# Two score phases per batch in place of four, with scores and transposes of the probabilities in the same four PSUM banks

## The chip, the core and the metric

The kernel runs on one NeuronCore of one Trainium2 chip. Its engines work from instruction streams of their own and meet at semaphores: TensorE (PE in the profile; its weight loads stand as PEld), VectorE (DVE), ScalarE (ACT), GpSimd (POOL) and SyncE (SP), which here only issues DMAs. The metric is the device time of one execution in microseconds, the median over several runs; lower is better.

## What is computed

64 graphs ("batches") of 256 nodes with 512 features, one 0/1 adjacency matrix for all. Two layers, each a residual with a layer norm behind it: a graph convolution, then masked attention with 8 heads of 64.

```python
def reference(x, adj, ...):
    # layer 0
    mi, mj = x @ Wi.T, x @ Wj.T
    a = adj.astype(x.dtype); deg = a.sum(axis=1)
    h = layernorm(x + deg[None, :, None] * (mi + b) + einsum('ij,bjo->bio', a, mj))
    # layer 1
    q, k, v = (split_heads(h @ W.T + bias) for W, bias in ((Wq, bq), (Wk, bk), (Wv, bv)))
    scores = where(adj == 0, -inf, einsum('bhqd,bhkd->bhqk', q, k) / 8)
    out = einsum('bhqk,bhkd->bhqd', softmax(scores), v)       # heads joined again
    return layernorm(h + out @ Wo.T + bo)
```

## The kernel before, in words

**Precision.** Every operand of a matmul is kept as two rounded halves, `_hi` and `_lo`; a product is three matmuls (hi·hi, lo·hi, hi·lo). ACT copies a PSUM result into the `_hi` half, DVE subtracts that from PSUM into the `_lo` half. `P` is 128, `R` = 2 row tiles of 128 nodes, `C` = 4 feature chunks, `G` = 4 pairs of heads; `g` counts the pairs.

**The step.** `steps` (L166) runs `step(b)` for b = 0 to 62, a loop of two steps a turn for most of them, and then `last_step(63)`. One step overlaps three batches: the attention of batch b, layer 0 and the projections q, k, v of batch n = b + 1, and the output projection y of batch b - 1. Every engine has its own list of calls for the step, written out by hand (PE L494, ACT L646, DVE L848, POOL L302). These lists and the semaphores set the order of everything; nothing schedules.

**PE.** `mj`, `mi` (L352, L363) multiply xT with two weights; `aggregate` (L370) applies the adjacency matrix; `transpose_h` (L404) turns the normalised h; `q`, `k`, `v`, `y` are projections of 12 matmuls of 512 columns (24 of 256 for a half of q or k). All of these write the three banks `proj`. `scores(b, g)` (L452) is 12 matmuls with 64 rows each, in six pairs that run side by side in the upper and the lower half of the array, one head in each; they fill the two banks `score`. `transpose_p(b, g, i)` (L469) turns the normalised probabilities of one head into bank `pt[i]`. `attend(b, g)` (L480) multiplies them with `v_both` into the bank `av`; it waits until `pt_low` (DVE, L791) has made both `pT_lo` of pair g, and until `o_sum` (L796) has read `av` of the pair before.

**The softmax of a pair.** `maxima` (DVE, L769: mask, row maxima, then `exp_bias`, a tensor_scalar), `exponentials` (ACT, L608), `inverse_sums` (DVE, L787), `normalise_even` (ACT, L618) and `normalise_odd` (POOL, L244), `transpose_p`, `pt_high` (ACT, L626), `pt_low`, `attend`, `o_low_part` (ACT, L633), `o_sum`, `o_high` (ACT, L640), `split_o` (POOL, L278).

**The norm of h.** `mi_sum`, `agg_sum` (DVE, L808, L817) add up h, `norm_stats` and `norm_mean` (L832, L836) take mean and variance, `root("h", n)` (POOL, L269) makes `rstd_h` with two small operations, and `norm_apply` (DVE, L842) scales the two row tiles of h with a tensor_scalar each (L845), from SBUF to SBUF. `transpose_h` waits for both.

**The next x.** `xT_high` and `split_xT` (POOL, L235, L251) make the two halves of xT for batch b + 2, one operation over 128x1024 elements each; their data is in SBUF a step early (`load_xT`, L183).

The calls between which the work around the change lies, on POOL and on DVE:

```python
305                normalise_odd(b, 0)
306                root("h", n)
307                normalise_odd(b, 1)
308                normalise_odd(b, 2)
309                if ahead: xT_high(b + 2)
310                if ahead: split_xT(b + 2)
...
862                norm_mean("h", n)
863                maxima(b, 2)
864                norm_apply("h", n, h_row)
```

## Time and profile before

| | |
|---|---|
| Median of 3 runs | 3143.62 us (3142.37 to 3143.76) |
| The profiled execution | 3145.57 us, its span 3143.7 us |
| PE busy | 3096.7 us, 99% of the span |
| DVE / ACT / POOL busy | 2298.9 / 1691.2 / 1148.2 us (73 / 54 / 37%) |
| Chain that ended last | PE 98%, DVE 1% |
| Granted TensorE clock, mean | 0.993 |

The profile is of one execution, from the first instruction to the last. A matmul's end in it is modelled: successive matmuls overlap, so the distance from start to start says how fast PE goes, not the duration of one. "Idle before <-releaser" is how long the engine stood before an instruction and what let it go on. A row with x2 merges two like instructions, its duration reaching from the start of the first to the end of the last.

### The profile page before, as it was taken

How to read it: one execution, taken by the hardware profiler on the slowest of the kernel's cores; microseconds unless marked ns; L12 is line 12 of the kernel's file. 1: busy time of each engine (PE TensorE's matmuls, PEld its weight loads, DVE VectorE, ACT ScalarE, POOL GpSimd, SP SyncE). 2: the span in 40 equal slices, each digit the busy share in tenths (PEclk: the TensorE clock that was granted, in tenths of full speed). 3: DMA queues.
4: the chain of work that ended last, by engine and by line, in shares of the span. 5: the costliest groups of instructions: out<-in, count | busy, mean ns of one | idle time of the engine just before them, and what ended most of it. 6: DMA issues, size and time to landing. Idle time of an engine off the chain costs nothing.

```text
span 3143.7 us, 60262 instructions
## 1 busy us (share of the span) xinstructions
PE 3096.7 (99%) x20480; PEld 2694.0 (86%) x20480; DVE 2298.9 (73%) x5644; ACT 1691.2 (54%) x4487; POOL 1148.2 (37%) x1097
## 2 busy tenths in 40 slices
PE   6999999999999999999999999999999999999997
PEld 5888888888888888888888888888888888888886
DVE  5677777777777777777777777777777777777776
ACT  3555555555555555555555555555555555555554
POOL 2343333333433333333334333333343333333332
PEclk8999999999999999999999999999999999999998
DMA  3011011010010110110101101101001011011010
GB/s 127 15 41 40 20 40 40 20 40 27 33 40 20 40 40 20 40 40 21 40 20 40 40 20 40 40 20 40 30 30 40 20 40 40 20 40 40 20 34 21
DMA packets 73002, 108.36 MB, mean 34 GB/s; under 512 B 3600, under 2 KB 36880, under 8 KB 72976
## 3 DMA queue, kind: packets, MB, share of 16 engines
q1 hardware_dynamic: 72976, 108.02, 10.4%
q8 instruction: 15, 0.25, 0.0%
q14 instruction: 11, 0.09, 0.0%
HBM read 74.46 MB, written 33.55 MB: 34 GB/s over the span
## 4 chain that ended last, share of the span: by engine, by line
PE 98%; DVE 1%; issue 0%; ACT 0%; DMA 0%; POOL 0%; POOLq 0%; DVEq 0%; SPq 0%; ACTq 0%
PE proj L337 73%; PE av L337 8%; PE pt L476 7%; PE score L463 7%; PE proj L414 2%; DMA probs<-in_w0T 0%; DVE h L845 0%; DVE probs L778 0%; DVE pT_lo L793 0%; DVE oT L802 0%; DVE wj_lo L897 0%; DVE wq_lo L897 0%; POOL var_eps_h L272 0%; DVE stats_out L834 0%; ACT probs L614 0%
## 5 line engine op out<-in xcount | busy, mean ns | idle before, releaser
L614 ACT ACTIVATE probs<-probs,exp_bias 128x256 f32<-128x256 f32 x1024 | 508.6, 498 | 374.5 <-DVE exp_bias L784 374.5
L280 POOL TENSOR_TENSOR oT_lo<-oT,oT_hi 128x256 fp32r<-128x256 f32 x256 | 189.2, 739 | 977.1 <-ACT oT_hi L644 977.1
L247 POOL TENSOR_TENSOR probs<-probs,row_inv 128x512 f32<-128x512 f32 x256 | 266.8, 1042 | 494.6 <-DVE row_inv L789 494.6
L778 DVE CUSTOM_DVE_ANT_0 probs<-score,mask_add 128x256 f32<-128x256 f32 x1024 | 371.4, 420 | 92.2 <-PE score L463 42.5
L630 ACT CAST pT_hi<-pt 128x512 fp32r<-128x512 f32 x512 | 280.1, 587 | 169.8 <-PE av L337 112.8
L793 DVE TENSOR_TENSOR pT_lo<-pt,pT_hi 128x512 fp32r<-128x512 f32 x512 | 333.5, 681 | 20.2 <-ACT pT_hi L630 16.2
L802 DVE SCALAR_TENSOR_TENSOR oT<-av,bv_cols,o_part 64x256 f32<-64x256 f32 x512 | 243.3, 475 | 97.2 <-ACT o_part L637 69.0
L784 DVE TENSOR_SCALAR exp_bias<-row_max 128x4 f32<-128x4 f32 x256 | 297.5, 1162 | 8.9
L623 ACT ACTIVATE probs<-probs,row_inv 128x256 f32<-128x256 f32 x512 | 234.2, 509 | 117.2 <-DVE row_inv L789 117.2
L337 PE MATMUL proj<-hT_hi,wq_hi 128*128 128x256 f32 x1024 | 289.2, 282 | 1.5 <-DVE hT_lo L739 1.5
L337 PE MATMUL proj<-hT_hi,wq_lo 128*128 128x256 f32 x1024 | 288.9, 282 | 0.0
L337 PE MATMUL proj<-hT_lo,wq_hi 128*128 128x256 f32 x1024 | 288.8, 282 | 0.0
L337 PE MATMUL proj<-hT_hi,wk_lo 128*128 128x256 f32 x1024 | 287.9, 281 | 0.0
L337 PE MATMUL proj<-hT_hi,wk_hi 128*128 128x256 f32 x1024 | 287.5, 281 | 0.0
L337 PE MATMUL proj<-hT_lo,wk_hi 128*128 128x256 f32 x1024 | 287.5, 281 | 0.0
L476 PE MATMUL pt<-ident,probs 128*128 128x128 f32 x2048 | 281.8, 276 | 2.1 <-ACT probs L623 2.1
L337 PE MATMUL av<-pT_hi,v_both 128*128 128x256 f32 x1024 | 272.0, 298 | 4.2 <-DVE pT_lo L793 4.2
L337 PE MATMUL av<-pT_lo,v_both 128*128 128x256 f32 x1024 | 256.0, 283 | 0.0
L476 PEld LDWEIGHTS pt<-ident,probs 128*128 128x128 f32 x2048 | 233.3, 141 | 20.1 <-ACT probs L623 2.6
L573 ACT CAST v_both<-proj 128x512 fp32r<-128x512 f32 x128 | 68.9, 590 | 334.6 <-PE av L337 330.5
L758 DVE SCALAR_TENSOR_TENSOR k_lo<-proj,bk_cols,k_hi 128x256 fp32r<-128x256 f32 x256 | 112.1, 479 | 169.4 <-ACT k_hi L598 169.4
L739 DVE TENSOR_TENSOR v_both<-proj,v_both 128x512 fp32r<-128x512 f32 x128 | 82.6, 686 | 208.0 <-ACT v_both L573 208.0
(100 smaller groups left out, 8897.3 us busy)
## 6 DMA issues: line engine op xcount, KB each, us to landing
xT_raw<-in_xT SPq DMA_DIRECT2D x64, 512.0 KB, 4.5
xb<-in_x SPq DMA_DIRECT2D x64, 512.0 KB, 5.3
out<-hb SPq DMA_DIRECT2D x64, 512.0 KB, 3.3
probs<-in_w0T SPq DMA_DIRECT2D x1, 1024.0 KB, 6.8
hb<-in_w0T SPq DMA_DIRECT2D x1, 1024.0 KB, 9.0
probs<-in_wqT SPq DMA_DIRECT2D x1, 1024.0 KB, 5.5
hb<-in_wkT SPq DMA_DIRECT2D x1, 1024.0 KB, 6.3
probs<-in_wvT SPq DMA_DIRECT2D x1, 1024.0 KB, 5.3
```

Source lines behind the costliest of these rows:

```text
L247: pool.tensor_tensor(probs[:, g % 2, 1, :, :], probs[:, g % 2, 1, :, :], row_inv[:, g % 2, R:2 * R].unsqueeze(2).to_broadcast([P, R, N]), ...
L280: pool.tensor_tensor(oT_lo[:, g, :], oT[:, :], oT_hi[:, g, :].bitcast(F32), ALU.subtract).then_inc(o_split, 1)
L337: return pe.matmul(dst, lhsT, rhs, start=start, stop=stop)
L463: last = pe.matmul(score[i][:, r * N:(r + 1) * N], q_[home, g, r * P:(r + 1) * P], k_[home, g, :], start=(r == 0 and j == 0), stop=(j == l ...
L476: last = pe.transpose(dst[:, kt, r * P:(r + 1) * P], probs[:, g % 2, i, r, kt * P:(kt + 1) * P], ident[:, :])
L614: last = nc.scalar.activation(e, e, ACT.Exp, bias=exp_bias[:, g % 2, s:s + 1], scale=SCALE, accum_out=row_sum[:, g % 2, s:s + 1])
L623: last = nc.scalar.activation(e, e, ACT.Copy, scale=row_inv[:, g % 2, r:r + 1])
L630: nc.scalar.copy(pT_hi[:, i, :, :], pt[i][:, :].rearrange("p (k q) -> p k q", k=R)).then_inc(pt_hi_done, 1)
L778: last = V.tensor_tensor_reduce(out=probs[:, g % 2, i, r, :], in0=score[i][:, r * N:(r + 1) * N], in1=mask_add[:, r, :], scale=1.0, scalar ...
L784: V.tensor_scalar(exp_bias[:, g % 2, :], row_max[:, g % 2, :], MAX_FLOOR, -SCALE, ALU.max, ALU.mult).then_inc(bias_done, 1)
L793: V.tensor_tensor(pT_lo[:, i, :, :], pt[i][:, :].rearrange("p (k q) -> p k q", k=R), pT_hi[:, i, :, :].bitcast(F32), ALU.subtract).then_in ...
L802: last = V.scalar_tensor_tensor(out=oT[i * HALF:(i + 1) * HALF, :], in0=av[0:HALF, i * N:(i + 1) * N], scalar=bv_cols[:, 2 * g + i:2 * g + ...
```

## The change

- The banks `score[0..1]` and `pt[0..1]` become four banks `attn[0..3]`. Pair g has the two banks `attn[2 * (g % 2) + i]`: first for its scores, then, once the probabilities have been read out, for its transposes. `pT_hi` and `pT_lo` get a second buffer for odd g. To make room, `hT_hi` and `hT_lo` take the place of `mj_hi` and `mj_lo`, which are dead when they are written.
- `scores(b, pair)` makes the scores of two pairs of heads, 24 matmuls in a row, so that a step has two score phases and not four: one in the place of the old first one, the other behind `attend(b, 1)`. It waits for `pt_low` of the pairs that had the banks before.
- On PE `y(b - 1, 0)` stands between the transposes of pairs 0 and 1, `y(b - 1, 1)` and `transpose_h` between `attend(b, 0)` and `attend(b, 1)`. q and k follow in a row behind the second score phase.
- ACT, DVE and POOL call the same functions in a new order. `last_step` is reordered in the same manner on all four engines (`scores(b, 0)`, y, pairs 0 and 1, y, `scores(b, 1)`, pairs 2 and 3).

No instruction that computes is added or taken away.

```diff
@@ -89,8 +89,9 @@
         mj_lo = sb("mj_lo", [P, R, D], F32R)
         h = sb("h", [P, R, D])
         hb = sb("hb", [P, 2, R, D])
-        hT_hi = sb("hT_hi", [P, C, N], F32R)
-        hT_lo = sb("hT_lo", [P, C, N], F32R)
+        hT_hi = mj_hi[:, :, :].rearrange("p r (a n) -> p (r a) n", a=2)
+        hT_lo = mj_lo[:, :, :].rearrange("p r (a n) -> p (r a) n", a=2)
@@ -100,8 +101,8 @@
         k_lo = sb("k_lo", [P, C, N], F32R)
         v_both = sb("v_both", [P, R, HEADS, 2 * DH], F32R)
         probs = sb("probs", [P, 2, 2, R, N])
-        pT_hi = sb("pT_hi", [P, 2, R, N], F32R)
-        pT_lo = sb("pT_lo", [P, 2, R, N], F32R)
+        pT_hi = sb("pT_hi", [P, 2, 2, R, N], F32R)
+        pT_lo = sb("pT_lo", [P, 2, 2, R, N], F32R)
         o_part = sb("o_part", [HALF, 2, N])
         oT = sb("oT", [P, N])
         oT_hi = sb("oT_hi", [P, G, N], F32R)
@@ -127,8 +128,8 @@
         proj = [bank(f"proj{i}") for i in range(3)]
-        score = [bank(f"score{i}") for i in range(2)]
-        pt = [bank(f"pt{i}") for i in range(2)]
+        attn = [bank(f"attn{i}") for i in range(4)]
         av = bank("av")
@@ -303,15 +304,15 @@
                 n = b + 1
                 add_bias(n)
                 normalise_odd(b, 0)
+                normalise_odd(b, 1)
                 root("h", n)
-                normalise_odd(b, 1)
-                normalise_odd(b, 2)
                 if ahead: xT_high(b + 2)
                 if ahead: split_xT(b + 2)
                 split_o(b, 0)
+                split_o(b, 1)
+                normalise_odd(b, 2)
                 normalise_odd(b, 3)
                 if y_: root("out", b - 1)
-                split_o(b, 1)
                 split_o(b, 2)
                 residual(n, 1 - parity, stored=y_)
                 split_o(b, 3)
...
@@ -449,28 +450,28 @@
                     pe.wait_ge(read["k"], 2 * n + 2)
                 rows_times_w("v", r, hT_hi, hT_lo, "wv")
-            def scores(b, g, first=False):
-                pe.wait_ge(read["q"], 2 * b + g // 2 + 1)
-                pe.wait_ge(read["k"], 2 * b + g // 2 + 1)
-                if not (first and g == 0):
-                    pe.wait_ge(max_done, 2 * (G * b + g))
-                terms = [(q_hi, k_hi), (q_lo, k_hi), (q_hi, k_lo)]
-                for r in range(R):
-                    for j, (q_, k_) in enumerate(terms):
-                        for i in range(2):
-                            home = slice(i * HALF, (i + 1) * HALF)
-                            last = pe.matmul(score[i][:, r * N:(r + 1) * N], q_[home, g, r * P:(r + 1) * P],
-                                             k_[home, g, :], start=(r == 0 and j == 0),
-                                             stop=(j == len(terms) - 1), skip_group_check=True)
-                            if r == R - 1 and j == len(terms) - 1:
-                                last.then_inc(score_done, 1)
-            def transpose_p(b, g, i, first=False):
+            def scores(b, pair, first=False):
+                pe.wait_ge(read["q"], 2 * b + pair + 1)
+                pe.wait_ge(read["k"], 2 * b + pair + 1)
+                if not (first and pair == 0):
+                    pe.wait_ge(pt_read, 2 * (G * b + 2 * pair))
+                for g in (2 * pair, 2 * pair + 1):
+                    terms = [(q_hi, k_hi), (q_lo, k_hi), (q_hi, k_lo)]
+                    for r in range(R):
+                        for j, (q_, k_) in enumerate(terms):
+                            for i in range(2):
+                                home = slice(i * HALF, (i + 1) * HALF)
+                                last = pe.matmul(attn[2 * (g % 2) + i][:, r * N:(r + 1) * N],
+                                                 q_[home, g, r * P:(r + 1) * P], k_[home, g, :],
+                                                 start=(r == 0 and j == 0), stop=(j == len(terms) - 1),
+                                                 skip_group_check=True)
+                                if r == R - 1 and j == len(terms) - 1:
+                                    last.then_inc(score_done, 1)
+            def transpose_p(b, g, i):
                 pe.wait_ge((norm_even_done, norm_odd_done)[i], G * b + g + 1)
-                if not (first and g == 0):
-                    pe.wait_ge(pt_read, 2 * (G * b + g) + i - 1)
-                dst = pt[i][:, :].rearrange("p (k q) -> p k q", k=R)
+                dst = attn[2 * (g % 2) + i][:, :].rearrange("p (k q) -> p k q", k=R)
                 for kt in range(R):
                     for r in range(R):
                         last = pe.transpose(dst[:, kt, r * P:(r + 1) * P],
...
@@ -497,32 +498,30 @@
                 scores(b, 0, not y_)
                 mj(n, 1)
                 mi(n, 0)
-                scores(b, 1)
                 mi(n, 1)
                 aggregate(n, 0)
                 aggregate(n, 1)
-                transpose_p(b, 0, 0, not y_)
-                transpose_p(b, 0, 1, not y_)
-                scores(b, 2)
+                transpose_p(b, 0, 0)
+                transpose_p(b, 0, 1)
                 if y_: y(b - 1, 0)
+                transpose_p(b, 1, 0)
+                transpose_p(b, 1, 1)
+                attend(b, 0, not y_)
                 if y_: y(b - 1, 1)
                 transpose_h(n, 0)
                 transpose_h(n, 1)
-                scores(b, 3)
-                transpose_p(b, 1, 0)
-                transpose_p(b, 1, 1)
-                attend(b, 0, not y_)
+                attend(b, 1)
+                scores(b, 1)
                 q(n, 0)
                 q(n, 1)
+                k(n, 0)
+                k(n, 1)
                 transpose_p(b, 2, 0)
                 transpose_p(b, 2, 1)
-                attend(b, 1)
-                k(n, 0)
-                k(n, 1)
+                v(n, 0)
                 transpose_p(b, 3, 0)
+                transpose_p(b, 3, 1)
                 attend(b, 2)
-                transpose_p(b, 3, 1)
-                v(n, 0)
                 v(n, 1)
                 attend(b, 3)
...
@@ -625,10 +622,11 @@
             def pt_high(b, g, i, first=False):
                 act.wait_ge(pt_done, 2 * (G * b + g) + i + 1)
-                if i == 0 and not (first and g == 0):
-                    act.wait_ge(av_done, G * b + g)
-                nc.scalar.copy(pT_hi[:, i, :, :],
-                               pt[i][:, :].rearrange("p (k q) -> p k q", k=R)).then_inc(pt_hi_done, 1)
+                if i == 0 and not (first and g < 2):
+                    act.wait_ge(av_done, G * b + g - 1)
+                nc.scalar.copy(pT_hi[:, g % 2, i, :, :],
+                               attn[2 * (g % 2) + i][:, :].rearrange("p (k q) -> p k q",
+                                                                     k=R)).then_inc(pt_hi_done, 1)
             def o_low_part(b, g, first=False):
                 act.wait_ge(av_done, G * b + g + 1)
@@ -648,36 +646,36 @@
                 mj_high(n, 0)
                 exponentials(b, 0)
                 mj_high(n, 1)
+                exponentials(b, 1)
                 normalise_even(b, 0)
-                exponentials(b, 1)
+                normalise_even(b, 1)
                 pt_high(b, 0, 0, not y_)
-                normalise_even(b, 1)
                 pt_high(b, 0, 1, not y_)
-                exponentials(b, 2)
+                o_low_part(b, 0, not y_)
+                pt_high(b, 1, 0, not y_)
+                pt_high(b, 1, 1, not y_)
                 hT_high(n, 0)
                 hT_high(n, 1)
+                o_low_part(b, 1)
+                o_high(b, 0, not y_)
+                exponentials(b, 2)
+                o_high(b, 1)
+                q_high(n, 0)
+                exponentials(b, 3)
                 normalise_even(b, 2)
-                pt_high(b, 1, 0)
-                pt_high(b, 1, 1)
-                o_low_part(b, 0, not y_)
-                exponentials(b, 3)
-                q_high(n, 0)
                 q_high(n, 1)
-                o_high(b, 0, not y_)
-                o_low_part(b, 1)
+                k_high(n, 0)
+                normalise_even(b, 3)
                 pt_high(b, 2, 0)
                 pt_high(b, 2, 1)
-                normalise_even(b, 3)
-                k_high(n, 0)
                 k_high(n, 1)
-                o_high(b, 1)
                 pt_high(b, 3, 0)
                 pt_high(b, 3, 1)
                 o_low_part(b, 2)
+                o_high(b, 2)
+                o_low_part(b, 3)
                 v_high(n, 0)
                 v_high(n, 1)
-                o_high(b, 2)
-                o_low_part(b, 3)
                 o_high(b, 3)
             def split_weight(i):
...
@@ -790,8 +789,9 @@
             def pt_low(b, g, i):
                 dve.wait_ge(pt_hi_done, 2 * (G * b + g) + i + 1)
-                V.tensor_tensor(pT_lo[:, i, :, :], pt[i][:, :].rearrange("p (k q) -> p k q", k=R),
-                                pT_hi[:, i, :, :].bitcast(F32), ALU.subtract).then_inc(pt_read, 1)
+                V.tensor_tensor(pT_lo[:, g % 2, i, :, :],
+                                attn[2 * (g % 2) + i][:, :].rearrange("p (k q) -> p k q", k=R),
+                                pT_hi[:, g % 2, i, :, :].bitcast(F32), ALU.subtract).then_inc(pt_read, 1)
             def o_sum(b, g, first=False):
@@ -847,50 +847,50 @@
             def step(b, parity, y_=True, ahead=True):
                 n, other = b + 1, 1 - parity
+                mj_low(n, 0)
                 maxima(b, 0, not y_)
-                mj_low(n, 0)
-                mi_sum(n, 0)
+                maxima(b, 1, not y_)
                 mj_low(n, 1)
                 inverse_sums(b, 0)
-                maxima(b, 1, not y_)
+                mi_sum(n, 0)
+                inverse_sums(b, 1)
                 mi_sum(n, 1)
                 agg_sum(n, 0)
                 agg_sum(n, 1)
                 norm_stats("h", n, 0, read["agg"], h_row)
                 norm_stats("h", n, 1, read["agg"], h_row)
-                inverse_sums(b, 1)
                 norm_mean("h", n)
-                maxima(b, 2)
+                pt_low(b, 0, 0)
+                pt_low(b, 0, 1)
                 norm_apply("h", n, h_row)
                 if y_: y_sum(b - 1, 0, other)
-                pt_low(b, 0, 0)
-                pt_low(b, 0, 1)
+                o_sum(b, 0, not y_)
+                pt_low(b, 1, 0)
+                pt_low(b, 1, 1)
                 if y_: y_sum(b - 1, 1, other)
-                inverse_sums(b, 2)
                 hT_low(n, 0)
                 hT_low(n, 1)
+                maxima(b, 2)
+                o_sum(b, 1)
                 maxima(b, 3)
+                q_low(n, 0)
                 if y_: norm_stats("out", b - 1, 0, read["y"], hb_row[other])
-                pt_low(b, 1, 0)
-                pt_low(b, 1, 1)
-                o_sum(b, 0, not y_)
+                inverse_sums(b, 2)
+                if y_: norm_stats("out", b - 1, 1, read["y"], hb_row[other])
+                if y_: norm_mean("out", b - 1)
                 inverse_sums(b, 3)
-                if y_: norm_stats("out", b - 1, 1, read["y"], hb_row[other])
-                q_low(n, 0)
                 q_low(n, 1)
-                o_sum(b, 1)
+                if y_: norm_apply("out", b - 1, hb_row[other])
+                k_low_half(n, 0)
                 pt_low(b, 2, 0)
                 pt_low(b, 2, 1)
-                if y_: norm_mean("out", b - 1)
-                k_low_half(n, 0)
                 k_low_half(n, 1)
                 pt_low(b, 3, 0)
+                pt_low(b, 3, 1)
                 o_sum(b, 2)
-                pt_low(b, 3, 1)
-                if y_: norm_apply("out", b - 1, hb_row[other])
+                o_sum(b, 3)
                 v_low(n, 0)
                 v_low(n, 1)
-                o_sum(b, 3)
             def split_weight(i):
                 dve.wait_ge(w_hi_done, i + 1)
...
```

What now stands in a row, at two places. **POOL, from `normalise_odd(b, 0)` (probs) through `root("h", n)` (var_eps_h, rstd_h) to the split of the next x (xT_hi, xT_lo).** Before:

```order
L247 TENSOR_TENSOR probs<-probs,row_inv 128x512
L271 ISA
L272 TENSOR_TENSOR var_eps_h<-mean_var_h,eps_cols 128x2
L275 TENSOR_TENSOR rstd_h<-var_eps_h,power_cols 128x2
L246 REGISTER_ALU
L247 TENSOR_TENSOR probs<-probs,row_inv 128x512
L246 REGISTER_ALU
L247 TENSOR_TENSOR probs<-probs,row_inv 128x512
L237 ISA
L239 REGISTER_ALU
L240 TENSOR_TENSOR xT_hi<-xT_raw,zero 128x1024
L253 TENSOR_TENSOR xT_lo<-xT_raw,xT_hi 128x1024
```

And after:

```order
L248 TENSOR_TENSOR probs<-probs,row_inv 128x512
L247 REGISTER_ALU
L248 TENSOR_TENSOR probs<-probs,row_inv 128x512
L272 ISA
L273 TENSOR_TENSOR var_eps_h<-mean_var_h,eps_cols 128x2
L276 TENSOR_TENSOR rstd_h<-var_eps_h,power_cols 128x2
L238 ISA
L240 REGISTER_ALU
L241 TENSOR_TENSOR xT_hi<-xT_raw,zero 128x1024
L254 TENSOR_TENSOR xT_lo<-xT_raw,xT_hi 128x1024
```

The two operations on xT stood behind two normalisations that had to wait for their pairs; now they stand right behind `rstd_h`.

**DVE, from the end of `maxima(b, 2)` (exp_bias) through `norm_apply` (h) to `hT_low`.** Before:

```order
L784 TENSOR_SCALAR exp_bias<-row_max 128x4
L845 TENSOR_SCALAR h<-h,mean_var_h,rstd_h 128x512 x2
L824 ISA
L826 TENSOR_TENSOR hb<-proj,hb 128x512
L793 TENSOR_TENSOR pT_lo<-pt,pT_hi 128x512 x2
L824 REGISTER_ALU
L826 TENSOR_TENSOR hb<-proj,hb 128x512
L788 REGISTER_ALU
L789 RECIPROCAL row_inv<-row_sum 128x4
L739 TENSOR_TENSOR hT_lo<-proj,hT_hi 128x512 x2
```

And after (`hT_lo` bears the name `mj_lo`, whose place it has taken):

```order
L840 BN_AGGR mean_var_h<-stats_h 128x2 x2
L792 TENSOR_TENSOR pT_lo<-attn,pT_hi 128x512 x2
L845 TENSOR_SCALAR h<-h,mean_var_h,rstd_h 128x512 x2
L824 ISA
L826 TENSOR_TENSOR hb<-proj,hb 128x512
L802 SCALAR_TENSOR_TENSOR oT<-av,bv_cols,o_part 64x256 x2
L792 TENSOR_TENSOR pT_lo<-attn,pT_hi 128x512 x2
L824 REGISTER_ALU
L826 TENSOR_TENSOR hb<-proj,hb 128x512
L737 TENSOR_TENSOR mj_lo<-proj,mj_hi 128x512 x2
```

`maxima(b, 2)` is gone from between `norm_mean` and `norm_apply`, and behind `norm_apply` now stand `o_sum(b, 0)` and the two `pt_low` of pair 1.

## Rows read from the trace of the kernel before

**Rows 1.** The page: busy time by engine, granted clock in 40 slices, the chain.
```profile
PE 3096.7 (99%) x20480; PEld 2694.0 (86%) x20480; DVE 2298.9 (73%) x5644; ACT 1691.2 (54%) x4487; POOL 1148.2 (37%) x1097
PEclk8999999999999999999999999999999999999998
PE 98%; DVE 1%; issue 0%; ACT 0%; DMA 0%; POOL 0%; POOLq 0%; DVEq 0%; SPq 0%; ACTq 0%
```

**Rows 2.** The chain in order of time: start us, us, what; two starts of `mj(n, 0)`.
```profile
1507.80 2.80 PE proj L337 x12
1510.60 0.91 PE score L463 x12
...
1523.06 0.87 PE pt L476 x8
...
1541.90 5.68 PE proj L337 x48
...
1555.95 2.80 PE proj L337 x12
```

**Rows 3.** Timeline of PE around `scores(b, 0)`: start us, us, engine, line, what.
```profile
1509.97 0.40 PE L337 MATMUL proj<-wj_hi,xT_lo 128*128 128x512 f32 x1
1510.20 0.39 PE L337 MATMUL proj<-wj_lo,xT_hi 128*128 128x512 f32 x1
1510.53 0.38 PE L463 MATMUL score<-k_hi,q_hi 64*128 64x256 f32 x2
1510.75 0.28 PE L463 MATMUL score<-k_hi,q_lo 64*128 64x256 f32 x2
...
1511.22 0.28 PE L463 MATMUL score<-k_lo,q_hi 64*128 64x256 f32 x2
1511.43 0.50 PE L337 MATMUL proj<-wj_hi,xT_hi 128*128 128x512 f32 x1
1511.77 0.39 PE L337 MATMUL proj<-wj_hi,xT_lo 128*128 128x512 f32 x1
```

**Rows 4.** Timeline of DVE and POOL in the same step, the norm of h.
```profile
1523.10 0.69 DVE L820 TENSOR_TENSOR h<-proj,h 128x512 f32<-128x512 f32 x1 [0.24 <-PE proj L337]
1525.09 0.31 DVE L840 BATCH_NORM_AGGREGATE mean_var_h<-stats_h 128x2 f32<-128x6 f32 x2
1525.76 0.70 POOL L275 TENSOR_TENSOR rstd_h<-var_eps_h,power_cols 128x2 f32<-128x2 f32 x1
1526.42 1.04 POOL L247 TENSOR_TENSOR probs<-probs,row_inv 128x512 f32<-128x512 f32 x1
1527.40 1.00 DVE L845 TENSOR_SCALAR h<-h,mean_var_h,rstd_h 128x512 f32<-128x512 f32 x2
1528.32 0.68 DVE L826 TENSOR_TENSOR hb<-proj,hb 128x512 f32<-128x512 f32 x1
1528.92 1.27 DVE L793 TENSOR_TENSOR pT_lo<-pt,pT_hi 128x512 fp32r<-128x512 f32 x2
1532.53 1.89 POOL L240 TENSOR_TENSOR xT_hi<-xT_raw,zero 128x1024 fp32r<-128x1024 f32 x1
1534.50 2.39 POOL L253 TENSOR_TENSOR xT_lo<-xT_raw,xT_hi 128x1024 fp32r<-128x1024 f32 x1
```

**Rows 5.** The same timeline later: `exp_bias` beside `xT_lo`, then `o_sum(b, 1)` and `pt_low`.
```profile
1535.09 1.83 DVE L784 TENSOR_SCALAR exp_bias<-row_max 128x4 f32<-128x4 f32 x1
1542.56 0.97 DVE L802 SCALAR_TENSOR_TENSOR oT<-av,bv_cols,o_part 64x256 f32<-64x256 f32 x2 [0.62 <-ACT o_part L637]
1543.56 1.29 DVE L793 TENSOR_TENSOR pT_lo<-pt,pT_hi 128x512 fp32r<-128x512 f32 x2
```

**Rows 6.** Timeline ahead of step 0: `root`, `norm_apply`, `xT_high(1)`, `split_xT(1)`.
```profile
33.99 0.70 POOL L275 TENSOR_TENSOR rstd_h<-var_eps_h,power_cols 128x2 f32<-128x2 f32 x1
34.66 1.89 POOL L240 TENSOR_TENSOR xT_hi<-xT_raw,zero 128x1024 fp32r<-128x1024 f32 x1
34.73 4.58 DVE L845 TENSOR_SCALAR h<-h,mean_var_h,rstd_h 128x512 f32<-128x512 f32 x2 [0.87 <-POOL rstd_h L275]
36.64 2.40 POOL L253 TENSOR_TENSOR xT_lo<-xT_raw,xT_hi 128x1024 fp32r<-128x1024 f32 x1
```

**Rows 7.** Stretches, us: PE, PEld, DVE, ACT, POOL busy, granted clock, DMA share, GB/s.
```profile
79.50:82.30 2.80, 0.00 (x0) 0.00 (x0) 2.74 (x14) 1.56 (x4) 1.91 (x3) 1.00 0.00 0
82.40:89.10 6.70, 6.06 (x32) 5.51 (x33) 3.82 (x10) 3.77 (x12) 4.54 (x3) 0.50 0.00 0
3097.80:3099.70 1.90, 0.00 (x0) 0.00 (x0) 1.51 (x4) 1.05 (x3) 1.36 (x2) 1.00 0.00 0
3099.80:3109.90 10.10, 6.01 (x34) 5.10 (x35) 4.96 (x24) 7.04 (x23) 4.48 (x5) 0.50 0.00 0
```

54 lines of the change are left out of this document (26 added, 28 removed).

## The prediction

> **What bounds the kernel now.** First the page: PE is busy 99% of the span, and the chain that ended last is 98% PE [rows 1]. In the chain in order of time a step runs from one `mj(n, 0)` to the next, 1507.80 to 1555.95: 48.15 us, every piece of it PE and none of it a wait [rows 2]. So a shorter step means either fewer microseconds of PE work, or nothing; and any wait that the new order puts in front of PE is paid in full. The granted clock is full in all slices but the first and the last [rows 1].
>
> **What the change takes away.** The timeline around `scores(b, 0)` shows what a score phase costs. Two 512-column matmuls start 0.23 us apart, the pairs of score matmuls 0.118 (1510.75 to 1511.22 over four). From the last `mj` matmul before the phase (1510.20) to the second one behind it (1511.77) are 1.57 us; without the phase it would be 2 x 0.233 = 0.47. The phase costs 1.10, its six pairs 6 x 0.118 = 0.71, and the rest, 0.39, is four gaps of about 0.1 where PE goes over from 128-row to 64-row matmuls and back (1510.20 to 1510.53, 1510.53 to 1510.75, 1511.22 to 1511.43, 1511.43 to 1511.77) [rows 3]. Four phases become two, and the 12 matmuls of the second pair then follow at 0.118 a pair: 2 x 0.39 = 0.78 us a step. The other matmuls and transposes are the same in number and kind, so PE's own work is 48.15 - 0.78 = 47.37 us a step. Over 63 steps that would be 49 us.
>
> **What it puts in.** I lay out the new step from the start of `mj(n, 0)` = 0, with the pieces of rows 2 and the distances of rows 3. PE: `mj(n, 0)` to 2.8, the score phase to 4.5, `mj(n, 1)`, `mi`, `aggregate` to 14.88, transposes of pair 0 to 15.75, `y(b-1, 0)` to 18.55, transposes of pair 1 to 19.42, `attend(b, 0)` to 20.37, `y(b-1, 1)` to 23.17, `transpose_h` to 24.04, and then `attend(b, 1)`, which needs the two `pt_low` of pair 1.
>
> DVE: `agg_sum(n, 1)` starts 0.20 behind the end of `aggregate` (before: 1523.10 against transposes from 1522.90 on), so at 15.08; from there to the end of `norm_mean` are 2.30 us [rows 4], 2.25 without the reciprocal that has moved away: 17.33. Then the two `pt_low` of pair 0, 1.27, whose data ACT has ready (transposes done at 15.9, two copies of 0.5): to 18.6.
>
> POOL: `rstd_h` ends 1.06 behind `norm_mean` (1525.40 to 1526.46) and POOL's next operation has started 0.04 before that [rows 4]. That next one is now `xT_high`. Nothing holds it: x lies ready since the step before, `mi` has ended at 13.2. So `xT_high` runs from 18.35 and `split_xT`, 1.97 behind it, from 20.32 to 22.71 [rows 4].
>
> `norm_apply` waits for `rstd_h`, so on DVE it can't start before 18.39, and meets `xT_high` in flight. What then happens stands in the prologue, where POOL and DVE have the same three calls in the same order: `xT_hi` starts 34.66, `norm_apply` 34.73, and its two instructions take 4.58 us and end at 39.31, 0.27 behind the end of `xT_lo` at 39.04 [rows 6]; undisturbed they take 1.00 [rows 4]. The tensor_scalar stands still while a POOL operation runs, and the second instruction comes behind the second operation. The loop has it too: `exp_bias`, four elements wide, takes 1.83 us and ends with `xT_lo` (1536.89) [rows 4, 5]. In the step of before `norm_apply` came between two POOL operations and nobody waited. By rows 6 the new one ends at 22.71 + 0.27 = 22.98.
>
> The Trainium skill has this as a rule (SBUF — State Buffer, section "Who interferes with whom"): VectorE in a two-port mode, which tensor_scalar can enter, and GpSimd take one pair of SBUF ports in turn, and the one that starts second blocks for the whole instruction. By that rule the 4.58 us of the prologue are no accident of the prologue; the trace agrees.
>
> Behind it on DVE are queued, at the spacings of rows 4 and 5: `y_sum` (starts 22.90, 0.60), `o_sum(b, 0)` (23.50, 1.00), two `pt_low` of pair 1 (24.50, 1.29), which end at 25.8. PE wants `attend(b, 1)` at 24.04 and starts it at 25.84, with its first weight load no longer hidden, some 0.05 more: **a wait of 1.85 us a step**. `transpose_h` itself gets its h (22.98 for 23.17) and its bank (`y_sum` ends 23.6, as needed) just in time.
>
> Bounds of this wait: nothing, if `norm_apply` slips through behind `xT_high` alone (then it ends near 20.8 and `pt_low` near 23.7); 2.4, if the half behind `y_sum` and the restart also cost. I take 1.85, since each term has its row and rows 6 are the same calls.
>
> **The rest of the step** I price at nothing, with this cover. `exp_bias` of pair 0 cost 2.38 us beside `add_bias` and may now find POOL free; what it gains nobody waits for. The transposes of pair 0, needed at 14.88, have their probabilities at about 12. The second half's chain (`maxima` of pair 2 about 1.1 behind the start of its phase, 1.5 us, exponentials 2.0, twice, then normalising) ends some 4 us before PE needs pair 2, behind q and k (2 x 5.7 us). `mj(n, 1)` at 4.5 needs `v_low`, now behind `o_sum(b, 3)`, at 3.1. `norm_apply` of "out" meets no POOL operation. `attend(b, 3)` has 1 us of room.
>
> **Sum.** Step: 47.37 + 1.85 = 49.22, which is 1.07 more than 48.15. 61 steps have it in full: 65 us. Step 62 has no next x to split (`ahead` is false): -0.8. Step 0 has no y (5.6 us less PE work), so its wait is about 5 us longer; before it waited 3.5 us and ran 6.7 us at half clock [rows 7] all the same: +3, between 0 and +6. The last step has less PE work between its score phase and pair 2, some +3, between -3 and +8. Together 65 - 0.8 + 3 + 3 = 70. The profiled execution took 3145.57 (span 3143.7 and 1.9 around it), so 3215.8; the median of the runs is 1.95 below it: **3214 us**.
>
> **Rivals.**
>
> - *The block isn't there, or is short* (one operation of POOL instead of two, or `norm_apply` first). For it: in the loop of before it never stood in `norm_apply`'s way. Against: POOL needs nothing but its own `rstd_h` to go on, while DVE must hear of it. Then PE doesn't wait at all, and the 49 us are saved: 3143.6 - 49 = 3095, **faster**. It decides from 0.8 us of wait a step downwards. Chance 0.14.
> - *The clock falls too.* A gap of 2.9 us without PE work ended with the clock at half for 6.7 us, and one of 1.9 us with 10 us of it [rows 7]. Mine is 1.7 to 1.8 us, behind a stretch of transposes. In 6.7 us at half clock PE does 3.4 us of work, so each fall costs 3.4. If it falls in 4 steps of 10: 0.4 x 61 x 3.4 = 83, so 3297; in all of them 3421. Against: the gap is the shortest of these, with work at full rate close around it. Chance 0.19. The Trainium skill (TensorE: Matmul & The Clock Gate, Part 4: PE-mode transpose) says that transposes don't count as activity for the clock. By that rule the quiet stretch would begin with `transpose_h`, 0.9 us earlier, and the sum would go towards the 3421 of a fall in every step; no run here has yet shown such a stretch.
> - *Another wait in the second half*, such as pair 2 late for its transposes or `mj(n, 1)` for `v_low`: at 1 us a step 61 more, 3275. The margins of 1.4 to 4 us speak against it. Chance 0.07.
>
> **How the numbers follow.** 0.60 for the forecast: 3190 (wait 1.5) to 3250 (2.4). 0.14 for 3095, 0.19 for the clock, most of it under 3310, 0.07 for a second wait. The range 3190 to 3310 leaves out the first rival and the worst of the second. A measurement of this kernel can tell 0.2% (6 us) from no change: slower by over that 0.84, the same 0.02, for a wait that just cancels the 0.78, faster 0.14.
>
> **What would show it.** In the timeline of DVE `norm_apply` (L845, h) takes over 4 us a step and ends 0.3 behind `xT_lo`; in the waits PE stands before `av` for `pT_lo` some 61 times, 1.6 to 1.9 us each; score phases stand twice a step, 24 matmuls in 1.4 us and four gaps of 0.1. Wrong if L845 stays at 0.54 us, if PE waits elsewhere, or if the granted clock shows halves inside the loop.

## The result and the profile after

| | us, median | runs | own time of the profiled execution | its span | granted clock |
|---|---|---|---|---|---|
| before | 3143.69 | 3142.37 to 3146.40 (4) | 3145.57 | 3143.7 | 0.993 |
| after | 3233.51 | 3230.72 to 3235.34 (4) | 3233.8 | 3232.0 | 0.991 |

The change makes the kernel **slower by 2.8%**: ratio 1.0284, 95% interval 1.0266 to 1.0302. The forecast was 3214, the range 3190 to 3310.

The page of after, busy time and chain as in [rows 1], with one group of its part 5:

```profile
PE 3082.5 (95%) x20480; PEld 2689.6 (83%) x20480; DVE 2266.2 (70%) x5644; ACT 1670.3 (52%) x4487; POOL 1159.1 (36%) x1097
PE 77%; DVE 16%; issue 6%; DMA 0%; ACT 0%; POOL 0%; DVEq 0%; SPq 0%; POOLq 0%
L845 DVE TENSOR_SCALAR h<-h,mean_var_h,rstd_h 128x512 f32<-128x512 f32 x128 | 294.3, 2339 | 0.9 <-POOL rstd_h L276 0.9
```

PE's busy time fell by 14 us (3096.7 to 3082.5) although the span grew by 88. So the time went into waits, and the chain that ended last says where: PE's share fell from 98% to 77%, DVE's rose from 1% to 16%. The third line names the suspect: one half of `norm_apply` takes 2339 ns on average, against 0.5 us in the loop of before [rows 4].

The waits of the whole execution (who waited <- for whom: us in total, times, longest):

```profile
PEld av L338 <- DVE pT_lo L792: 112.9, 64, 1.8
PE av L338 <- DVE pT_lo L792: 99.1, 65, 1.8
PEld proj L415 <- DVE hb L826: 10.8, 61, 0.2
```

Once a step PE's matmul waits 1.5 us for `pt_low` (99.1/65), and its weight load 1.8 (112.9/64). The third row is a small wait that the prediction held to be none: 61 times 0.18 us, in `transpose_h`, for the bank that `y_sum` empties. It delays the last four transposes; PE has to wait for `pt_low` right behind them in any case.

The chain through one step, and on to the next `mj(n, 0)` (start us, us, what):

```profile
1548.26 2.80 PE proj L338 x12
1551.06 1.62 PE attn L465 x24
...
1568.53 1.91 DVE h L845
...
1573.27 0.69 DVE pT_lo L792
1574.01 1.22 PE av L338 x8
...
1597.66 2.80 PE proj L338 x12
```

A step takes 1597.66 - 1548.26 = **49.40 us**, against 48.15 [rows 2]. In the middle the chain leaves PE for DVE: `h` (`norm_apply`), later `pT_lo`, and back to PE with `av`. The score phase is 24 matmuls in one piece of 1.62 us, where there were 12 in 0.91.

The timeline of DVE and POOL at that place, a step earlier, with two rows of PE, the transposes of h and the first matmul of `attend(b, 1)` (in brackets at a row's end: the wait ahead of it and for whom):

```profile
1515.76 0.25 DVE L840 BATCH_NORM_AGGREGATE mean_var_h<-stats_h 128x2 f32<-128x6 f32 x2
1515.92 1.26 DVE L792 TENSOR_TENSOR pT_lo<-attn,pT_hi 128x512 fp32r<-128x512 f32 x2
1516.36 0.70 POOL L276 TENSOR_TENSOR rstd_h<-var_eps_h,power_cols 128x2 f32<-128x2 f32 x1
1517.03 1.89 POOL L241 TENSOR_TENSOR xT_hi<-xT_raw,zero 128x1024 fp32r<-128x1024 f32 x1
1517.10 4.66 DVE L845 TENSOR_SCALAR h<-h,mean_var_h,rstd_h 128x512 f32<-128x512 f32 x2
1519.00 2.47 POOL L254 TENSOR_TENSOR xT_lo<-xT_raw,xT_hi 128x1024 fp32r<-128x1024 f32 x1
1521.68 0.68 DVE L826 TENSOR_TENSOR hb<-proj,hb 128x512 f32<-128x512 f32 x1
1522.28 0.96 DVE L802 SCALAR_TENSOR_TENSOR oT<-av,bv_cols,o_part 64x256 f32<-64x256 f32 x2
1523.27 1.29 DVE L792 TENSOR_TENSOR pT_lo<-attn,pT_hi 128x512 fp32r<-128x512 f32 x2
...
1521.86 1.21 PE L415 MATMUL proj<-ident,h 128*128 128x128 f32 x8
1524.61 0.39 PE L338 MATMUL av<-pT_hi,v_both 128*128 128x256 f32 x1 [1.54 <-DVE pT_lo L792]
```

Read it from the fourth row. `xT_hi` starts on POOL at 1517.03; `norm_apply` is ready 0.07 later (1517.10) and needs 4.66 us for its two instructions; it ends at 1521.76, 0.29 behind the end of `xT_lo` (1519.00 + 2.47 = 1521.47). Then come `y_sum`, `o_sum(b, 0)` and the two `pt_low` of pair 1, with nothing between them, until 1524.56, and 0.05 later PE starts `attend(b, 1)`. These are the 4.58 us and the 0.27 of the prologue of before [rows 6], now 62 times in the loop. Between the start of PE's last transpose and that of the first `av` matmul lie 1.79 us more than in the first experiment below, where nothing holds `av` up; with the 0.16 by which the last transpose itself is late, `attend(b, 1)` starts 1.95 us later there.

**Where the 88.3 us of span went** (3232.0 - 3143.7). Ahead of step 0: +0.7. Step 0: +0.6 (49.49 against 48.90). 61 steps of the loop at 49.40 against 48.15: +76. Four of these steps took 50.9, since the granted clock fell in them: +6. Step 62 and the last step, from the last `mj(n, 0)` to the last matmul: +5.2 (91.96 against 86.74). Behind the last matmul: -0.4.

One of the four falls (windows: PE, PEld, DVE, ACT, POOL busy, granted clock, DMA share, GB/s):

```profile
482.70:484.20 1.50, 0.00 (x0) 0.00 (x0) 1.47 (x4) 0.59 (x1) 0.00 (x0) 1.00 0.00 0
485.90:489.20 3.30, 3.30 (x26) 3.08 (x23) 2.35 (x12) 1.09 (x5) 0.73 (x1) 0.50 0.00 0
489.30:493.00 3.70, 3.70 (x33) 3.70 (x33) 2.19 (x12) 2.97 (x12) 0.74 (x1) 1.00 0.00 0
```

The gap stands first, with PE idle at the upper level of 2.4 GHz; 1.7 us behind it begins a stretch of 3.4 us at 0.50, which is 1.2 GHz, and then the clock is back. The falls begin at 485.85, 1277.74, 2069.64 and 2861.53 us, in every 16th step. The loop of before has none behind step 0.

### The profile page after: what moved, and what is told of

Read it like the earlier page. It is cut to its first block, busy times and chain, and to the rows that moved or that the text cites. A ratio compares the mean times of both kernels' runs of the same rounds, so it can differ in the third digit from the quotient of the medians.

```text
span 3232.0 us, 59563 instructions
## 1 busy us (share of the span) xinstructions
PE 3082.5 (95%) x20480; PEld 2689.6 (83%) x20480; DVE 2266.2 (70%) x5644; ACT 1670.3 (52%) x4487; POOL 1159.1 (36%) x1097
## 3 DMA queue, kind: packets, MB, share of 16 engines
q1 hardware_dynamic: 72976, 108.02, 10.1%
## 4 chain that ended last, share of the span: by engine, by line
PE 77%; DVE 16%; issue 6%; DMA 0%; ACT 0%; POOL 0%; DVEq 0%; SPq 0%; POOLq 0%
PE proj L338 60%; PE attn L465 6%; PE av L338 6%; DVE pT_lo L792 5%; DVE h L845 4%; PE attn L477 4%; DVE stats_h L834 2%; DVE oT L802 2%; DVE h L820 1%; DVE hb L826 1%; DVE mean_var_h L840 0%; DMA hb<-in_w0T 0%; DMA xb<-in_x 0%; ACT probs L611 0%; POOL xb L259 0%
## 5 line engine op out<-in xcount | busy, mean ns | idle before, releaser
L627 ACT CAST pT_hi<-attn 128x512 fp32r<-128x512 f32 x512 | 275.8, 590 | 424.9 <-PE attn L477 423.4
L792 DVE TENSOR_TENSOR pT_lo<-attn,pT_hi 128x512 fp32r<-128x512 f32 x512 | 328.0, 682 | 213.7 <-ACT pT_hi L627 211.7
L777 DVE CUSTOM_DVE_ANT_0 probs<-attn,mask_add 128x256 f32<-128x256 f32 x1024 | 372.8, 421 | 54.7 <-PE attn L465 44.0
L338 PE MATMUL av<-pT_hi,v_both 128*128 128x256 f32 x1024 | 274.7, 300 | 102.6 <-DVE pT_lo L792 99.1
L338 PE MATMUL proj<-mj_hi,wq_hi 128*128 128x256 f32 x1024 | 296.9, 290 | 1.5 <-DVE mj_lo L737 1.5
L338 PEld LDWEIGHTS av<-pT_hi,v_both 128*128 128x128 f32 x1024 | 195.6, 191 | 121.8 <-DVE pT_lo L792 112.9
L845 DVE TENSOR_SCALAR h<-h,mean_var_h,rstd_h 128x512 f32<-128x512 f32 x128 | 294.3, 2339 | 0.9 <-POOL rstd_h L276 0.9
L338 PE MATMUL proj<-mj_lo,wq_hi 128*128 128x256 f32 x1024 | 289.7, 283 | 0.0
L338 PE MATMUL proj<-mj_hi,wq_lo 128*128 128x256 f32 x1024 | 289.6, 283 | 0.0
L338 PE MATMUL proj<-mj_hi,wk_hi 128*128 128x256 f32 x1024 | 287.7, 281 | 0.0
L338 PE MATMUL proj<-mj_hi,wk_lo 128*128 128x256 f32 x1024 | 287.7, 281 | 0.0
L338 PE MATMUL proj<-mj_lo,wk_hi 128*128 128x256 f32 x1024 | 287.7, 281 | 0.0
L477 PE MATMUL attn<-ident,probs 128*128 128x128 f32 x2048 | 267.4, 274 | 9.4 <-ACT probs L620 5.4
L477 PEld LDWEIGHTS attn<-ident,probs 128*128 128x128 f32 x2048 | 238.4, 141 | 36.0 <-ACT probs L620 6.1
```

The lines of the kernel that those rows point to most:

```text
L338: return pe.matmul(dst, lhsT, rhs, start=start, stop=stop)
L477: last = pe.transpose(dst[:, kt, r * P:(r + 1) * P], probs[:, g % 2, i, r, kt * P:(kt + 1) * P], ident[:, :])
L627: nc.scalar.copy(pT_hi[:, g % 2, i, :, :], attn[2 * (g % 2) + i][:, :].rearrange("p (k q) -> p k q", k=R)).then_inc(pt_hi_done, 1)
L777: last = V.tensor_tensor_reduce(out=probs[:, g % 2, i, r, :], in0=attn[2 * (g % 2) + i][:, r * N:(r + 1) * N], in1=mask_add[:, r, :], scal ...
L792: V.tensor_tensor(pT_lo[:, g % 2, i, :, :], attn[2 * (g % 2) + i][:, :].rearrange("p (k q) -> p k q", k=R), pT_hi[:, g % 2, i, :, :].bitca ...
L845: V.tensor_scalar(row(r), row(r), mean_var[which][:, r, 0:1], rstd[which][:, r:r + 1], ALU.subtract, ALU.mult).then_inc(normed[which], 1)
```

## The experiments

The theory: `norm_apply` meets the two operations on the next x in POOL and stands still until the second has ended; all the loss hangs on that, and all the gain of having two phases fewer (0.78 us a step by the prediction) is there underneath. The rivals: the new order of DVE itself makes `pt_low` late (more work ahead of it, whatever POOL does), or the phases gave nothing.

### The two operations on x only when norm_apply has ended

```
                 root("h", n)
+                if ahead: pool.wait_ge(normed["h"], R * (n + 1))
                 if ahead: xT_high(b + 2)
                 if ahead: split_xT(b + 2)
```

> The changed kernel with one wait more on POOL: xT_high(b+2) starts only when both norm_apply of h are done. Nothing else moves. Theory A (POOL's two operations on xT hold up the tensor_scalar of norm_apply, and through it pT_lo of pair 1 and PE's attend(b, 1)): L845 on h falls from 2.1 and 2.6 us to 0.54 each, PE's 1.8 us wait before av goes away altogether, a step takes 47.4 us instead of 49.4, and the time is 3095 to 3106 us, under the kernel before. Theory B (the new order of DVE is simply too long between norm_mean and pT_lo of pair 1, whatever POOL does): the wait stays over 1 us a step and the time over 3190.

Measured: **3106.59** (3105.61 to 3107.36), ratio to before 0.9882, interval 0.9865 to 0.9898. Its timeline at the same place:

```profile
1551.54 1.00 DVE L846 TENSOR_SCALAR h<-h,mean_var_h,rstd_h 128x512 f32<-128x512 f32 x2
1552.46 0.68 DVE L827 TENSOR_TENSOR hb<-proj,hb 128x512 f32<-128x512 f32 x1
1552.78 1.90 POOL L241 TENSOR_TENSOR xT_hi<-xT_raw,zero 128x1024 fp32r<-128x1024 f32 x1 [1.27 <-DVE h L846]
1554.75 2.40 POOL L254 TENSOR_TENSOR xT_lo<-xT_raw,xT_hi 128x1024 fp32r<-128x1024 f32 x1
1555.32 1.29 DVE L793 TENSOR_TENSOR pT_lo<-attn,pT_hi 128x512 fp32r<-128x512 f32 x2
```

and two starts of its first score phase, in the chain:

```profile
1536.11 1.62 PE attn L466 x24
1583.54 1.62 PE attn L466 x24
```

`norm_apply` takes 1.00 us, POOL waits 1.27 for it, and nobody waits for POOL. The step is 47.43 us in all 61, PE has no wait in the loop, and the clock doesn't fall there. One line in another engine's program turns 2.8% slower into 1.2% faster: the theory stands. With the order of DVE unchanged, `pt_low` is in time, so the first rival falls. The step is 48.15 - 47.43 = 0.72 us shorter than before, so the second falls too; whether that comes from the phases is tried further down. What this kernel doesn't win is the end: from the last `mj(n, 0)` to the last matmul 93.9 us, against 86.7 before.

### One operation in the way instead of two

```
                 if ahead: xT_high(b + 2)
+                if ahead: pool.wait_ge(normed["h"], R * (n + 1))
                 if ahead: split_xT(b + 2)
```

> The changed kernel, but only split_xT waits for norm_apply; xT_high still starts right behind rstd_h. Theory A: norm_apply now loses only the time of one operation, its first instruction takes 2.1 us and its second 0.54, pT_lo of pair 1 ends near 23.7 of the step, just ahead of the 24.0 at which PE wants it, and PE doesn't wait: 3095 to 3110 us. If the second operation were harmless (the block is by the first alone), nothing would change: 3233.

Measured: **3106.03** (3105.81 to 3108.83), ratio 0.9884, interval 0.9867 to 0.9900.

```profile
1552.58 2.56 DVE L846 TENSOR_SCALAR h<-h,mean_var_h,rstd_h 128x512 f32<-128x512 f32 x2
```

`norm_apply` takes 2.56 us, 1.6 more than alone, and the step is 47.43 as well: PE has the room for one blocked operation, not for two. This is the bound "nothing" of the prediction, brought about. It also shows what the 4.66 consist of: the first half comes when `xT_hi` ends; with no second operation behind it, the other half follows at once. With one behind it, the other half stands still once more, for the whole of it (2.11 us and 2.63 us for the two halves of after, 2.11 and 0.54 here).

### The meeting alone, in the kernel before

The kernel before with its four phases, and only the two operations on x moved to where the change has them:

```
                 root("h", n)
-                normalise_odd(b, 1)
-                normalise_odd(b, 2)
                 if ahead: xT_high(b + 2)
                 if ahead: split_xT(b + 2)
+                normalise_odd(b, 1)
+                normalise_odd(b, 2)
```

> The kernel before with its order of PE, ACT and DVE, and on POOL xT_high and split_xT moved to right behind root(h, n), as the change has them. Theory A: exp_bias of pair 2 waits for xT_hi, norm_apply of h for xT_lo (L845 about 3 us longer), transpose_h comes 1.1 us a step late and the time is 3185 to 3250 us (3211 if 1.1 us a step). Theory B (the loss belongs to the new order): within 5 us of 3144.

Measured: **3214.11** (3212.96 to 3215.41), ratio 1.0223, interval 1.0206 to 1.0240; the steps take 49.21 and 49.29 us in turn (one of the 61 takes 49.5), and the clock doesn't fall in them.

```profile
1511.35 1.89 POOL L240 TENSOR_TENSOR xT_hi<-xT_raw,zero 128x1024 fp32r<-128x1024 f32 x1
1512.05 1.22 DVE L784 TENSOR_SCALAR exp_bias<-row_max 128x4 f32<-128x4 f32 x1
1513.18 3.07 DVE L845 TENSOR_SCALAR h<-h,mean_var_h,rstd_h 128x512 f32<-128x512 f32 x2
1513.32 2.65 POOL L253 TENSOR_TENSOR xT_lo<-xT_raw,xT_hi 128x1024 fp32r<-128x1024 f32 x1
```
```profile
PE proj L414 <- DVE h L845: 60.1, 63, 10.1
```

With the old phases, the old banks and the old place of the output projection the same move costs 1.10 us a step on average. The way of it is a little different, and tells something: `exp_bias`, four elements wide, is the one that is blocked by `xT_hi` (1.22 us, to 1513.27, 0.03 behind the end of `xT_hi`); then the first half of `norm_apply` slips in ahead of `xT_lo` (0.54 us, from 1513.18), and the second is blocked. `xT_lo` pays for it with 2.65 us, against 2.39 [rows 4]. PE waits for h itself: of the 60.1 us 10.1 lie ahead of step 0 and 6.4 in step 0, which leaves 43.6 / 61 = 0.7 us a step. So what makes the kernel slow is one of the change's edits, and not the one that its description names.

### Is it the lock, or being late at all?

DVE waits by a semaphore until both operations are through, so that neither half of `norm_apply` runs or stands beside one of them:

```
                 pt_low(b, 0, 1)
+                if ahead: dve.wait_ge(xT_split, b + 3)
                 norm_apply("h", n, h_row)
```

> The changed kernel with a wait more on DVE: norm_apply of h starts only when split_xT is done, so that both its instructions run behind xT_lo (one of them ran between the two POOL operations). Theory A: h is ready 0.75 us later, PE waits that much more, spread over transpose_h and attend(b, 1): 61 x 0.75 = 46 us, 3275 to 3285. The clock: in the changed kernel it fell in 4 of 62 steps at a gap of 1.54 us. If a longer gap brings it down more often, each fall of 3.4 us at half clock adds 1.7: falls in half the steps would give 3330.

Measured: **3326.36** (3317.25 to 3328.10), ratio 1.0572, interval 1.0554 to 1.0590. PE's two waits in a step:

```profile
1514.69 1.25 PE L415 MATMUL proj<-ident,h 128*128 128x128 f32 x8 [0.48 <-DVE h L845]
1517.49 0.39 PE L338 MATMUL av<-pT_hi,v_both 128*128 128x256 f32 x1 [1.54 <-DVE pT_lo L792]
```

The steps without a fall take 50.1 us, 0.7 more than after: the second half of `norm_apply` is no longer all but done when POOL ends, and PE waits 0.48 for h. The wait for `pt_low` stays at 1.54, since its chain behind h is as long as it was. That is the delay as such, and it answers the question: PE loses what h and `pt_low` come late, whether DVE is blocked or waits of its own accord. The rest of the loss is the clock: it fell in 35 of the 61 steps, where after had 4 (steps of 50.1 us: 26; 51.5 and 51.6: 31, with a fall of 3.4 us each; 52.9: 4, with falls of 6.8). Of the 93 us between this kernel and after, 61 x 0.7 = 43 are the delay, and about 31 x 1.45 + 4 x 2.8 - 6 = 50 the falls.

### A longer gap behind the same transposes

`y_sum(b-1, 1)` is moved ahead of the `pt_low` of pair 1 in DVE, which makes the gap behind the transposes longer and puts none ahead of them:

```
                 o_sum(b, 0, not y_)
+                if y_: y_sum(b - 1, 1, other)
                 pt_low(b, 1, 0)
                 pt_low(b, 1, 1)
-                if y_: y_sum(b - 1, 1, other)
```

> The changed kernel with y_sum(b-1, 1) ahead of pT_lo of pair 1 on DVE instead of behind it. pT_lo of pair 1 comes 0.6 us later and the one gap of PE before attend(b, 1) grows from 1.54 to 2.14 us; the transposes of h stay unbroken. By the wait alone 61 x 0.6 = 37 us more: 3270. The clock fell in 4 steps with the gap of 1.54, and in 37 steps of e4_both_after_lo, with gaps of 0.47 and 1.54 around the transposes. If the length of the gap decides, it now falls in at least as many steps as there, and at 1.4 us a fall the time is 3315 or more; if the broken transposes were what mattered, it stays near 3270.

Measured: **3350.19** (3347.68 to 3350.94), ratio 1.0656, interval 1.0638 to 1.0673: the first of the two cases, in which the length of the gap is enough, with the transposes unbroken. (The 37 steps of the expectation are 35, as counted above.)

```profile
188.34 0.58 PE L338 MATMUL av<-pT_hi,v_both 128*128 128x256 f32 x1 [2.14 <-DVE pT_lo L792]
```
```profile
186.30:188.10 1.80, 0.00 (x0) 0.00 (x0) 1.77 (x4) 0.52 (x1) 0.00 (x0) 1.00 0.00 0
188.20:191.50 3.30, 3.16 (x18) 2.94 (x20) 1.28 (x3) 0.89 (x2) 0.08 (x1) 0.50 0.03 5
191.60:236.00 44.40, 44.40 (x295) 39.08 (x294) 30.35 (x80) 23.77 (x66) 17.86 (x17) 1.00 0.11 36
```

The gap is 2.14 us, and a fall comes in 53 of 61 steps, which begins between 0.3 us before the gap ends and 1.5 us behind that. It lasts 3.4 us and adds 1.4 to 1.5 us (51.5 against 50.0); in three steps it lasts 6.8. The three kernels side by side:

| kernel | PE's gaps around the transposes of h, us | steps with a fall, of 61 | clock over the span |
|---|---|---|---|
| after | 1.54 behind them | 4 | 0.991 |
| DVE waits for both | 0.48 ahead, 1.54 behind | 35 | 0.972 |
| longer gap | 2.14 behind | 53 | 0.963 |

The second row has the same longest gap as the first, and nine times as many falls. What differs is the 0.48 ahead of the eight transposes. So the longest gap alone doesn't order the three kernels; the plain sum of the gaps (1.54, 2.02, 2.14) does.

The rule that the prediction cites (the Trainium skill, TensorE: Matmul & The Clock Gate, Part 4: PE-mode transpose) is that transposes don't count as activity. By that rule the transposes and the gaps around them are one quiet stretch. The traces agree in part: from where the transposes could start to the first matmul of `av` it is 2.7 us long in after, 3.4 in the second kernel and 3.3 in the third. The two longer ones bring far more falls, but the longest is not the one with the most, so the rule stays unproven here.

### What a score phase costs

The first experiment's kernel, with its second phase cut in two by `q(n, 0)`:

```
-                scores(b, 1)
+                scores(b, 1, only=0)
                 q(n, 0)
+                scores(b, 1, only=1)
                 q(n, 1)
```

> e1_x_after_norm with its second score phase cut in two: the scores of pair 2, then q(n, 0), then the scores of pair 3. Same matmuls, one phase more in a step. If a phase costs four gaps of 0.1 us beyond its pairs, as read from the profile of before (0.39), a step takes 47.43 + 0.39 = 47.82 us and the time is 3106.6 + 62 x 0.39 = 3131 us (3127 to 3135). If what the merge of the phases gained came from elsewhere (the new order), the time stays at 3107. If pair 3, whose chain starts 2.9 us later, comes late, more than 3140.

Measured: **3130.85** (3129.87 to 3131.68), ratio 0.9958, interval 0.9942 to 0.9975. In its chain:

```profile
1522.38 0.91 PE attn L466 x12
1523.29 3.04 PE proj L339 x24
1526.33 0.91 PE attn L466 x12
```

The step grows from 47.43 to 47.83 us, 0.39 to 0.40 for one more phase. Undoing half of the change's gain costs half of it back (the two phases removed had given 0.36 each), so the 0.39 read from four gaps of 0.1 us [rows 3] is the price of a phase, going from 128-row to 64-row matmuls and back, at both places where it was measured.

### The same meeting ahead of the loop

The prologue has it too [rows 6], in both kernels. The first experiment's line, there as well:

```
             root("h", 0)
+            pool.wait_ge(normed["h"], R)
             xT_high(1)
             split_xT(1)
```

> e1_x_after_norm, and in the prologue xT_high(1) waits for norm_apply of h(0) as well. There L845 took 4.6 us between two operations of POOL with PE idle behind it; without the block 1.0 us. The whole program behind it starts 3.6 us earlier: 3103.0 us. If something else (the split of wv, which DVE makes there) is late next: 3106.

Measured: **3103.00** (3101.75 to 3104.31), ratio 0.9872, interval 0.9856 to 0.9889, against 3106.59 without it. The waits:

```profile
PE proj L417 <- DVE h L847: 6.5, 1, 6.5
```

PE's wait for the first h fell from 10.1 to 6.5 us, and step 0 begins 4.6 us earlier (57.5 for 62.1). Step 0 itself then takes 1.3 longer (49.4 for 48.1). The difference of the medians, 3.6 us, is the one expected. The profiled spans differ by more, 5.6 us (3105.5 to 3099.9), and the half clock of both ends is in that. In step 0 this trace has 10.2 us at half clock, for 6.8 in the first experiment's. At the end it is the other way round: from the last `mj(n, 0)` to the last matmul the first two experiments took 93.9 and 91.5 us with the same code, with 23.9 and 17.1 us at half clock, and this one 91.5 with 17.1.

### The last step

The page of the first experiment's kernel shows PE waiting 3.5 us once for a normalisation by POOL in the last step. Moved ahead of a split:

```
                 split_o(b, 0)
-                split_o(b, 1)
                 normalise_odd(b, 2)
+                split_o(b, 1)
```

> e6_prologue_too, and in the last step POOL normalises pair 2 before it splits o of pair 1. In e1_x_after_norm the transposes of pair 2's second head waited 3.5 us for that normalisation (POOL was waiting for ACT's oT_hi, which stood behind the exponentials of pair 3). Without that wait 3 to 3.5 us less than e6_prologue_too: 3099.5 us, the fastest of all. If ACT or DVE are as late for pair 2 as POOL was, 3102.

Measured: **3101.33** (3099.39 to 3101.74), ratio 0.9863, interval 0.9847 to 0.9880. The profiled spans with and without it are the same, 3099.9 us. First the waits of the kernel without it, then with it:

```profile
PE av L340 <- DVE pT_lo L794: 6.0, 4, 1.8
PE attn L479 <- ACT probs L622: 5.4, 2, 3.6
PE attn L479 <- POOL probs L248: 4.0, 1, 4.0
```
```profile
PE av L340 <- DVE pT_lo L794: 8.0, 4, 3.4
PE attn L479 <- ACT probs L622: 5.4, 2, 3.6
```

POOL's row is gone, and `pt_low` has taken half of its place: 2.0 us more, and the longest wait there is 3.4 us now for 1.8. ACT's row stands as it was. So 2.0 of the 4.0 us came back (in the profiled execution 3.4 us more at half clock took most of that away), and the medians differ by 1.7. The expectation of 3099.5 was missed; what came is near its other case, 3102, with DVE the one that is late next. It is nonetheless the fastest kernel that was run: 1.4% under before, 4.1% under after.

## Why the prediction was right

**What bounds the kernel.** Right: with PE at 99% and a chain without a wait, every wait that the order put ahead of PE was paid in full. PE's busy time went down and the time up.

**PE's own work, 47.37 us a step.** It is 47.43, by the 61 steps of the first experiment. Two phases less give 0.72 and not 0.78; a term right to 0.06.

**The lock.** Right, and nearly to the digit, because the prologue had the same three calls: `norm_apply` 4.66 us (4.58 there), ended 0.29 behind `xT_lo` (0.27 there). In the prediction's own time, from the start of `mj(n, 0)` (at 1498.70 us in this trace), it was to end at 22.98 and ended at 23.06. The choice of "slips through behind `xT_high` alone" would have been wrong, and the second experiment shows what it would have given: no wait at all, 3106 us. The rival at 3095 was this one. It didn't come about; brought about, it gives 3106 and not 3095, of which 0.06 x 63 = 4 us are the phases and most of the rest the end of the kernel (+4.8 us in that experiment, +7.1 in the first).

**The wait, 1.85 us.** Right in kind and place, and a little too small: it is 1.97, from 49.40 - 47.43. (The sign was 1.6 to 1.9 us each; the trace shows 1.54 for the matmul and 1.8 for its weight load.) The end of `pt_low` sets it, and DVE has no gap from `norm_apply` to there; so what counts is when `pt_low` ends and when PE could have started `attend(b, 1)`. `norm_apply` ended 0.08 late, and everything behind it with it: `y_sum` at 23.66 for 23.6, `attend(b, 1)` started at 25.91 for 25.84. And PE could have started it at 23.96, as in the first experiment, for 24.04. The step that failed in its own terms is "`transpose_h` itself gets its h and its bank just in time": the bank came too late, and the last four transposes were held up by 0.16 us in each of the 61 steps (the third row of the waits). By the order of the calls that cost nothing more, since `pt_low` doesn't depend on these transposes and PE would have stood the same 0.16 us ahead of `attend(b, 1)`; this is read from the trace, no run tried it. By the sum the step is 47.43 + 1.97 = 49.40, predicted 47.37 + 1.85 = 49.22. Over 61 steps the 0.18 are 11 of the 18 us by which the sum was short (3215.8 against 3233.8): 7 of the wait and 4 of PE's own work.

**The clock.** Its own rival with 0.19. It was not what made the loss, and yet it happened a little: 4 of 61 steps, 6 us. "The granted clock shows halves inside the loop" was one of the prediction's signs of being wrong, and this one did show. The price put on a fall was wrong: 3.4 us. That supposed that PE loses half of the 6.7 us seen beside [rows 7]; in the loop a fall is 3.4 us long, and the step with it is 1.5 longer. By the right price the rival with a fall in 4 of 10 steps would have been 37 us and not 83. The fourth and the fifth experiment show how near it stood: with 0.48 us of gap more, 35 steps of 61; with 0.6 more, 53. To call a gap of 1.8 safe since 1.9 and 2.9 were not was thin.

**Another wait in the second half.** None: nothing but the waits ahead of and behind the last transposes stands in the steady step, and the first experiment has no wait of PE in the loop at all.

**The ends.** Step 0 and what lies ahead of it were priced at +3 and gave 1.3. The last step at +3, with -0.8 for step 62, gave +5.2 together, so about +6 alone, inside its bounds of -3 to +8. So the shortfall is 7 of the wait, 4 of PE's own work, 6 of the clock, and 6 - 3 - 1.7 = 1 of the ends. The chain in the last step passes through `attn L477`, waiting for `probs` of ACT (5.4 us in 2 waits) and of POOL (4.0 in one), with too little PE work left to put over them. The longest waits of the last step, 3.55 us ahead of `attend(b, 0)` and 3.6 and 4.0 for `probs` of pair 2, add up with the shorter ones to 17.1 us in which PE stands idle behind the last `mj(n, 0)`, against 10.4 before. As for the clock, both traces have the same time at half clock there (17.07 us), so it isn't that: 6.7 us more of waits, less 1.4 for the phases saved in step 62 and the last step, make the 5.2. The chain there:

```profile
3184.08 2.09 ACT probs L611 x8
3186.41 0.92 ACT probs L620 x2
3187.37 1.09 PE attn L477 x8
3188.46 3.55 issue
3192.01 2.05 PE av L338 x8
```

Of these waits only the one for POOL was tried, and half of it came back. What a better order of the last step would give stays open.

## What to carry to other kernels

Before an operation is moved, ask what it will meet on the other engines at its new place, not only who waits for it: here a split of x, for which nobody waited at either place, cost 127 us (4%) by standing beside a tensor_scalar on the path, and turned a gain of 1.2% into a loss of 2.8%. Where the kernel has the same calls in the same order elsewhere, in a prologue say, the trace of before has the price already. A good regrouping and a bad move can lie in one change. One wait on the engine that has time to spare (POOL waits 1.3 us, PE none) parted them and turned 3233.5 into 3106.6 us.
